# A fused block on one core: first loads in pieces, taps by turns, other orders in the slots, fewer waits

## The reference, cut to what matters

```python
# x: 4 x 512 x 512, ctx: 4 x 512 x 256, all f32
def mixer(hidden, z):                       # a selective scan (Mamba) on the context
    x = einsum('bld,ed->bel', hidden, in_proj_w)
    x = silu(causal_conv4(x, conv_w) + conv_b)          # 4 taps per channel
    dt_low, B, C = split(einsum('bdl,ed->bel', x, x_proj_w), [16, 32])
    dt = softplus(einsum('brl,dr->bdl', dt_low, dt_proj_w) + dt_proj_b)
    # for t: state = state * exp(dt*A) + dt*x*B ; y = sum_n state*C   (16 states n)
    y = (y + D * x) * silu(z)
    return swapaxes(y, 1, 2)
x = x + tanh(g_xattn) * mixer(ctx, layernorm(x))
# bitlinear: rms norm, 8-bit rounding of rows, weights rounded to -1, 0, 1
h = silu(bitlinear(layernorm(x), w1)) * bitlinear(layernorm(x), w2)      # 2048 wide
x = x + tanh(g_ffn) * bitlinear(h, w3)
```

## Time and profile before

| what | us |
|---|---|
| median of 3 executions | 670.55 (667.59 to 671.76) |
| the profiled execution | 668.04 |
| its span, first to last instruction | 666.0 |
| POOL busy in the span | 595.4 (89%) |
| DVE busy | 578.7 (87%) |
| ACT busy | 538.8 (81%) |
| PE busy | 500.3 (75%) |

### The profile page before, as it was taken

How to read it: one execution, slowest core, us unless ns; L and a number is a source line. 1 busy time by engine, 2 the same in 40 slices (tenths; PEclk the granted TensorE clock), 3 DMA queues, 4 the chain that set the end, 5 groups by cost and what they waited for, 6 DMA issues and landing times.

```text
span 666.0 us, 8112 instructions
## 1 busy us (share of the span) xinstructions
PE 500.3 (75%) x2562; PEld 307.0 (46%) x2562; DVE 578.7 (87%) x766; ACT 538.8 (81%) x995; POOL 595.4 (89%) x292
## 2 busy tenths in 40 slices
PE   8868978876553768787675667678686877778897
PEld 3234534443452445554553445354463545446454
DVE  7678976958899799999988899999997999999764
ACT  5763766689999779988697797899899898987774
POOL 1399999999899999999999999999999999999321
PEclk9879999999566979999785999899999998989999
DMA  5597676558970000148420100028620000000000
GB/s 182 189 407 294 233 283 253 196 215 346 414 294 0 19 20 1 48 137 273 132 81 1 32 0 17 1 95 269 210 76 1 16 1 17 0 17 17 0 32 31
DMA packets 23929, 80.77 MB, mean 121 GB/s; under 512 B 2432, under 2 KB 4608, under 8 KB 20816
## 3 DMA queue, kind: packets, MB, share of 16 engines
q1 hardware_dynamic: 23888, 80.27, 33.3%
HBM read 72.53 MB, written 7.73 MB: 121 GB/s over the span
## 4 chain that ended last, share of the span: by engine, by line
DVE 32%; ACT 32%; PE 21%; issue 12%; DMA 2%; POOL 1%; SPq 0%; DVEq 0%; ACTq 0%; POOLq 0%
DVE hh L769 9%; DVE hh L766 8%; ACT da L731 6%; PE bank_b L316 5%; ACT da L738 3%; DVE room L1040 3%; PE bank_y L847 3%; ACT room L1033 2%; ACT room L1179 2%; PE bank_a L241 2%; DVE sm L1087 2%; ACT wq L674 2%; ACT room L1053 2%; PE bank_a L1006 2%; PE da L1199 2%
## 5 line engine op out<-in xcount | busy, mean ns | idle before, releaser
L769 DVE TENSOR_TENSOR_SCAN hh<-da,hh 128x1024 f32<-128x1024 f32 x89 | 202.3, 2279 | 5.1 <-ACT da L738 3.9
L847 PE MATMUL bank_y<-ident,hh 128*128 128x128 f32 x1024 | 144.3, 290 | 10.7 <-POOL hh L814 9.9
L809 POOL TENSOR_TENSOR hh<-hh,cc 128x1024 f32<-128x1024 f32 x61 | 145.4, 2385 | 0.6 <-DVE hh L766 0.6
L847 PEld LDWEIGHTS bank_y<-ident,hh 128*128 128x128 f32 x1024 | 128.8, 151 | 33.4 <-issue 12.6
L814 POOL TENSOR_TENSOR hh<-hh,cc 128x1024 f32<-128x1024 f32 x59 | 140.3, 2378 | 0.0
L703 POOL TENSOR_TENSOR hh<-pair,bb 128x1024 f32<-128x1024 f32 x30 | 70.9, 2364 | 29.1 <-DMA bb<-xd_scratch 24.6
L766 DVE TENSOR_TENSOR_SCAN hh<-da,hl,hh 128x256 f32<-128x256 f32 x124 | 82.7, 729 | 0.0
L703 POOL TENSOR_TENSOR hh<-wq,bb 128x1024 f32<-128x1024 f32 x32 | 76.1, 2383 | 1.3 <-PE bank_y L847 1.3
L697 POOL TENSOR_TENSOR hh<-wq,bb 128x1024 f32<-128x1024 f32 x32 | 76.2, 2384 | 0.9 <-PE bank_y L847 0.9
L697 POOL TENSOR_TENSOR hh<-pair,bb 128x1024 f32<-128x1024 f32 x32 | 76.2, 2389 | 0.4 <-PE bank_y L847 0.4
L316 PE MATMUL bank_b<-room 128*128 128x512 f32 x96 | 46.0, 623 | 19.0 <-DVE wq L420 19.0
(11 more groups left out here) (262 smaller groups left out, 1050.3 us busy)
## 6 DMA issues: line engine op xcount, KB each, us to landing
bb<-xd_scratch SPq DMA_DIRECT2D x32, 512.0 KB, 5.1
cc<-xd_scratch SPq DMA_DIRECT2D x32, 512.0 KB, 7.4
wq<-weights SPq DMA_DIRECT2D x12, 1024.0 KB, 6.1
stage<-weights SPq DMA_DIRECT2D x8, 1024.0 KB, 6.1
xin<-x SPq DMA_DIRECT2D x4, 1024.0 KB, 5.4
room<-weights SPq DMA_DIRECT2D x4, 1024.0 KB, 7.2
u_scratch<-wq SPq DMA_DIRECT2D x6, 512.0 KB, 3.1
wq<-x SPq DMA_DIRECT2D x2, 1024.0 KB, 17.9
```

The costliest lines, as they stand in the source:

```text
L769: ins = v.tensor_tensor_scan(to, da, h, 0.0, ALU.mult, ALU.add)
L809: ins = g_.tensor_tensor(quarters(flat(hh[k % NH])), quarters(flat(hh[k % NH])), cc[:, n:n + 4, t], ALU.mult)
L847: mm = pe.matmul(bank_y[:, (first + c) * P:(first + c + 1) * P], flat(hh[k % NH])[:, at:at + P], ident[:, :], start=False, stop=(s == STEP ...
```

## The change

- The first loads: the context of batch 0 in two halves and the projection weights as a first quarter (the 128 columns of channel block 0) and the rest, the halves and the quarter issued first, consts third. `in_proj` of block 0 waits for the half that it is about to read, that of block 1 for the rest of the weights. `warm` is called with 2 in place of 3.
- The taps: in place of three taps of block 0, three of block 1 and so on, DVE does them by turns, so that from the fourth tap on two taps of one block have mostly one of another block between them. `diag_w` of blocks 2 and 3 and `pick` are made behind the taps, not ahead of them.
- `BY_VECTOR` goes from 8 steps to 9: (12, 15 | 45, 52, 63, 67, 73 | 120) becomes (11 | 45, 51, 53, 62, 67, 68, 73, 77 | none), the bars standing for the three stretches.
- `PAIR` of 2 goes from slot 26 to 25, `round_slot` of 6 from 27 to 28, two z slots by one; weight part 0 is rounded by DVE instead of ACT.
- The order within the slots changes on PE, DVE, ACT and POOL in all three stretches, and in the end; in the last stretch the centring of rows stands between the two halves of `exp`.
- Some 220 waits go which another wait implies: about 129 on ACT, 88 on DVE; none on POOL.

```diff
-PAIR = {2: 26, 3: 37, 4: 49, 5: 64, 6: 87, 7: 99}
+PAIR = {2: 25, 3: 37, 4: 49, 5: 64, 6: 87, 7: 99}
-BY_VECTOR = (12, 15, 45, 52, 63, 67, 73, 120)
+BY_VECTOR = (11, 45, 51, 53, 62, 67, 68, 73, 77)
...
         def in_proj(pe, b, e, bank):
             for k in range(KC):
+                if b == 0 and e == 0:
+                    pe.wait_ge(*d_ctx0[k].of("all"))
...
         def first_front_vector(v):
-            for e in range(NE):
-                v.wait_ge(*FA.of(("ev", 0, e)))
...
-                for k in (2, 1, 0):
-                    if k < 2:
-                        v.wait_ge(*FV.now())
...
+            for e, k in ((0, 2), (0, 1), (0, 0), (1, 2), (1, 1), (2, 2), (1, 0), (2, 1), (3, 2), (2, 0), (3, 1), (3, 0)):
+                if k == 2:
+                    v.wait_ge(*FA.of(("ev", 0, e)))
...
+                else:
+                    v.wait_ge(*FV.of(("tap", e, k + 1)))
...
         def round_slot(i):
-            return (20, 21, 23, 24, 25, 26, 27, 29, 30, 32, 33, 35)[i]
+            return (20, 21, 23, 24, 25, 26, 28, 29, 30, 32, 33, 35)[i]
...
         def rounded_by_scalar(i):
-            return i in (0, 1, 3, 7, 9, 10)
+            return i in (1, 3, 7, 9, 10)
...
         def gated_vector(v, i, c):
...
-            if i >= 2:
-                v.wait_ge(*MP.of(("hT", i - 2, c)))
...
+                d_ctx0[0].did(sp.dma_start(ctx_sb[0][:, 0, :], ctx_t[0, :, 0, :]), "all")
+                d_w[0].did(sp.dma_start(ipw[:, :, 0:P], in_w[:, :, 0:P]), "all")
                 d_const.did(sp.dma_start(cst[:, 0:94], consts), "all")
-                load_ctx(0)
-                d_w.did(sp.dma_start(ipw, in_w), "all")
+                d_ctx0[1].did(sp.dma_start(ctx_sb[0][:, 1, :], ctx_t[0, :, 1, :]), "all")
+                d_w[1].did(sp.dma_start(ipw[:, :, P:DM], in_w[:, :, P:DM]), "all")
...
             def _(pe):
                 pe.wait_ge(*PV.of("spare"))
-                warm(pe, 3, bank_y)
-                pe.wait_ge(*d_ctx[0].of(0))
-                pe.wait_ge(*d_w.of("all"))
+                warm(pe, 2, bank_y)
+                pe.wait_ge(*d_w[0].of("all"))
                 for e in range(NE):
+                    if e == 1:
+                        pe.wait_ge(*d_w[1].of("all"))
```

In the end, ACT's list (before, and after):

```diff
                 center_scalar(act, 15, 1)
+                rows_scalar(act, 14, 1)
                 xr_scalar(act, 14)
-                rows_scalar(act, 14, 1)
                 square_end(act, 13, 1)
                 tanh_scalar(act, 13, 3)
                 square_end(act, 13, 2)
+                xqt_scalar(act, 14)
                 square_end(act, 13, 3)
-                xqt_scalar(act, 14)
...
                 tanh_scalar(act, 15, 3)
+                hqt_scalar(act, 14, 1)
                 square_end(act, 15, 2)
-                hqt_scalar(act, 14, 1)
                 square_end(act, 15, 3)
```

and PE's, where the third product of tile 13 goes behind the first two chunks of tile 15:

```diff
-                out_tensor(pe, 13)
                 ab_tensor(pe, 15, 0)
                 ab_tensor(pe, 15, 1)
+                out_tensor(pe, 13)
                 ab_tensor(pe, 15, 2)
```

More of the change, by code:

```diff
@@ L1383, in _ @@
                             cfac_pool(g_, first, n)
+                    if k < ALL and not c_by_vector(k):
+                        times_c(g_, k)
                     if k + LEAD < ALL:
@@ L1563, in _ @@
                             dt_scalar(act, 2 * n + 1)
+                    for i in range(END - 1):
+                        if k == tile_slot(i) + 9:
+                            hqt_scalar(act, i, 2)
                     for i in range(END + 1):
@@ L1599, in _ @@
                             z_scalar(act, i)
+                    for i in range(END + 1):
+                        if k == tile_slot(i) - 1:
+                            xqt_scalar(act, i)
                     for b in range(NB):
@@ L1669, in _ @@
                 for k in range(0, 38):
+                    for i in range(END + 1):
+                        if k == tile_slot(i) - 1:
+                            xt_tensor(pe, i)
                     if 0 <= k - 1 < ALL:
@@ L1683, in _ @@
                             z_turn_tensor(pe, i)
+                for k in range(38, 80):
+                    if 0 <= k - 1 < ALL:
+                        sums(pe, k - 1)
                     for i in range(END + 1):
@@ L1686, in _ @@
                             xt_tensor(pe, i)
-                for k in range(38, 80):
                     for i in range(END - 1):
@@ L1690, in _ @@
                             ht_tensor(pe, i, 2)
-                    if 0 <= k - 1 < ALL:
-                        sums(pe, k - 1)
+                    for i in range(END - 1):
+                        if k == tile_slot(i) + 10:
+                            out_tensor(pe, i, (0, 1))
                     for i in TILES:
@@ L1825, in _ @@
                 v.wait_ge(*PV.now())
-                for e in range(NE):
+                for e in (0, 1):
                     for j in range(TAPS):
@@ L1832, in _ @@
                     PV.did(v.tensor_copy(pick[:, n, :], ident[:, at:at + 1].to_broadcast([P, P])), "pick")
-                v.wait_ge(*PV.now())
-                first_front_vector(v)
+                for e in (2, 3):
+                    for j in range(TAPS):
+                        PV.did(v.tensor_scalar(diag_w[:, e, j, :], ident[:, :], cw[:, e, j:j + 1], None, ALU.mult),
+                               "diag_w")
                 du_vector(v, 0)
@@ L1843, in _ @@
                 for k in range(0, 38):
+                    for first, n, done in TURNS:
+                        if k == done + 2:
+                            for i in range(first, first + n):
+                                stats_vector(v, i)
+                            for i in range(first, first + n):
+                                aggr_vector(v, i)
                     if k + LEAD - 1 < ALL:
@@ L1893, in _ @@
                         times_c_vector(v, k + LEAD - 1)
+                    for first, n, done in TURNS:
+                        if k == done + 3:
+                            rows_vector(v, first, n)
                     for i in range(END):
@@ L1915, in _ @@
                                 aggr_vector(v, i)
+                    for i in range(END):
+                        if k == tile_slot(i) + 4:
+                            peak_vector(v, i, 1)
                     for i in range(END - 1):
@@ L1921, in _ @@
                             z_vector(v, i)
+                    for i in range(END):
+                        if k == tile_slot(i) + 2:
+                            peak_vector(v, i, 0)
+                    for n in PAIR:
+                        if k == PAIR[n]:
+                            du_vector(v, 2 * n)
+                            du_vector(v, 2 * n + 1)
                 for k in range(80, SLOTS):
@@ L1929, in _ @@
                             gated_vector(v, i, c)
+                    for first, n, done in TURNS:
+                        if k == done + 2:
+                            for i in range(first, first + n):
+                                stats_vector(v, i)
+                            for i in range(first, first + n):
+                                aggr_vector(v, i)
+                    for i in range(END):
+                        if k == tile_slot(i) + 5:
+                            scales_vector(v, i, 0)
                     if k % STEPS == 0 and PER < k <= ALL:
@@ L1973, in _ @@
                 rows_vector(v, 14, 1)
+                hqt_vector(v, 12, 3)
                 hqt_vector(v, 12, 2)
```

330 lines of the change are left out of this document (135 added, 195 removed).

## The result

| | before | after |
|---|---|---|
| median | 670.53 us (667.59 to 673.45, 12 executions) | 666.99 us (663.35 to 668.98, 12 executions) |
| ratio | | 0.994, 95% interval 0.9923 to 0.9958 |
| profiled execution, its span | 668.04, 666.0 | 667.88, 666.1 |

By the ratio the change makes the kernel 4.0 us faster (2.8 to 5.2; the medians are 3.5 apart), where 8.6 were forecast. 666.99 lies inside the wide range of 655.5 to 670, but 5 us above the predicted 662.0 and outside the forecast's own range of 658 to 666. One execution of 1237.7 us, of a kernel of the experiments, is left out everywhere.

What follows compares the result with a forecast made beforehand. POOL, never pausing from 213 to 500 us, was taken to set the pace; -1.6 - 1.5 - 5.5 + 1.5 - 1.5 = -8.6 us from 670.55 gave 662.0, own range 658 to 666, eight in ten within 655.5 to 670.

Steps and rivals of the forecast that it cites:

- Waits: On DVE and ACT, none on POOL: removing waits that others imply gives 0 us, range 0 to -1.
- First front: Before POOL's first product: earlier block 0 gives 1.1 us, taps by turns 0.5; sum -1.6, bounds 0 and -2.4.
- Slots 0 to 37: First stretch: one more POOL product, +2.32, against pauses giving back about 3.8; sum -1.5, bounds +2.3 and -3.5.
- the credit for part 0: Slots 0 to 37: weight part 0 rounded by DVE takes 2.09 us off ACT before the z turn, shortening POOL's pauses.
- Slots 38 to 79: Middle: three products fewer save POOL 7.0 us, less 1.5 of new pauses; sum -5.5, bounds 0 and -7.0.
- Slots 80 to the last product by C: Late stretch: step 120 back on POOL, +2.32, its last pauses (1.3 and 0.6) halved; sum +1.5, bounds +0.5 and +2.9.
- The end: Behind POOL's last product, 47 us: shorter PE waits give -0.7 and -0.8; sum -1.5, bounds +1 and -3.
- with the first gain passed on: In the end: the -0.7 from PE's first two waits carries on, and tile 14's shorter wait adds another -0.8.
- The first (668.2): Rival, chance 0.27: the middle saves only part, as half of DVE's idle time stays; -2.3 us, 668.2.
- The second: Rival, chance 0.08: DVE takes over the pace in slots 38 to 79, its idle time staying; +6.4 us, 677.
- The third: Rival, chance 0.12: all POOL pauses go (-7.7), front gives 2.4, net product 2.3, end 2.5; -14.9 us, 656.
- the fourth: Rival: load pieces come no earlier and tap turns do nothing; -7.0 us, 663.5, inside the forecast's own range.

Runs made afterwards that it cites:

- the pair run side by side: Changed kernel with the some 220 waits put back, second time, 666.67 us (0.9936 to before), beside the unaltered changed kernel, 666.79 us (0.9943).
- the first run: Changed kernel with the some 220 waits put back, nothing else, first time: 664.66 us, ratio 0.9911 to the kernel before.

## Why the prediction was wrong, and where it held

**Waits: right.** Forecast 0; 0.1 us in the pair run side by side, and in the first run no loss from the waits either.

**First front: right mechanism, half the size.** -1.6 forecast, -0.8 measured. The step that failed is "block 0 is done at 7.2 against 8.3, a gain of 1.1". Block 0 is done at 7.59, since `warm` lost its two fast matmuls and gave 0.91 us in place of 1.6, and this isn't what the later work hangs on: the prediction followed block 0 and did not ask when the rest of the weights, issued later and in smaller packets, would let block 1 go. Block 1 starts 0.4 us earlier. The taps by turns gave 0.33 to 0.50 where 0.5 was forecast; their two pitches were read rightly.

**Slots 0 to 37: wrong.** -1.5 forecast, +0.3 measured, or -0.3 without the b10 pause, which differs from execution to execution. The sentence that failed is "in 156 to 213 us ACT has 55.54 of 57 us busy [...] so there ACT paces", and with it the credit for part 0: given back to ACT, it changes nothing, and part 7 taken off ACT and given to DVE made the stretch longer. PE's wait at the z turn fell to 6.07 us, as forecast (near 6), and POOL had nothing of it. The other half of the step, that an added product costs +2.32 and pauses are a gain to be had beside it, failed too: two products more for POOL and two fewer for DVE left the stretch at 187.57. The pauses (the b10 pause left out) did fall, from 5.1, 7.0 and 5.4 us to between 2.9 and 3.5, but because the added product fills them. The z turn's pause went from 1.8-2.6 to 0.9-1.5, and `y_keep`, 3.8 us later now, makes a new one of 1.2 to 1.5. That is the term where most was lost, 1.8 of the 4.7 us, or 1.2 without the b10 pause.

**Slots 38 to 79: the number right by luck, the mechanism half seen.** -5.5 forecast, -5.2 measured, with 1.2 to 2.5 us of pauses in place of 1.5, DVE at 94 of 100 us from 300 to 400 where 96 to 98% was forecast. That POOL's list paces it, at 2.32 us for a product, holds. Unseen was that the list without the orders costs 3.5 us and the orders without the list 2.5 to 3. The step that failed is that the prediction took the new orders of this stretch at nothing; beside the new list they are worth 6 to 8 us of pauses. It came out right by taking the new pauses at 1.5, which it had no row for.

**Slots 80 to the last product by C: mis-sized.** +1.5 forecast, +2.6 measured. The product adds its 2.32 of work to POOL's list; "which I expect to halve", of the pauses there, failed: they went from about 2.0 to 2.2 us. With the old late orders and step 120 by DVE the stretch is as long, and with the same product behind a DVE without products it costs nothing. That DVE comes out of the middle later with more behind it would explain both; no run tests it apart from the rest, and the cause stays open.

**The end: mis-sized.** -1.5 forecast, -0.7 measured. The waits came near to what was taken: the first two are gone, the "about 0.3" that the row scales give back is 0.6, and the second wait went by 0.75 of 0.8. What failed is "with the first gain passed on": of 1.25 us won by the product of tile 14, 0.5 are lost to PE's waits for tile 15, whose rounding on ACT comes only 0.23 us earlier.

**The rivals.** The first (668.2) came nearest to the total, for another reason than its own: the middle saved nearly all, the rest did not. The second is what the list would do alone. The third fell. So did the fourth, though only half of the front's gain came.

## What to carry to other kernels

A high busy share says that an engine could pace a stretch, not that it does: ACT at 97% was relieved of 2.1 us in favour of DVE, and the stretch grew by 1.7, because the waits ran through DVE and PE's fixed order. A pause of the engine that seems to pace may be one that more work only fills: two products more in slots 0 to 37 cost nothing. A list that shifts work and an order that shifts waits can each be a loss and together a gain, so try them both ways before one is thrown out. When a load is cut in pieces, follow the last piece too, since the second consumer waits for that one.

## What the runs showed of the hardware

One and the same place of one kernel runs with TensorE at either clock level from execution to execution, and the eight matmuls that take 5.37 us in place of 3.67 reach POOL, through PE's sums, as some 2 us more of pause. So two single profiles can differ by more than the whole effect here: two of the changed kernel span 666.1 and 661.9 us, and those of before and after first shown 666.0 and 666.1, for medians 3.5 us apart. Issuing one load on SP took 0.38 to 0.65 us, so the fifth leaves 2.2 us behind the first. Waits that another implies, some 220 of them, cost nothing that can be measured. The taps, DVE operations on 128x512 f32, start 0.79 us apart when each needs the one before, and 0.66 to 0.67 when it does not.
